# The mixture-of-experts block of layer 0 and the addition of its rows, one attention chunk earlier

## The reference

```
x = L0_attn_x
xn = _layernorm(x, axis=-1)
x = x + _L0_attn_ref(xn, ...) + _L0_ffn_ref(xn, ...)
xn = _layernorm(x, axis=-1)
x = x + _L1_attn_ref(xn, ...) + _L1_ffn_ref(xn, ...)
```

## Time and profile before

| | |
|---|---|
| median of three runs | 444.68 us (440.51 to 448.02) |
| profiled execution | 446.3 us, of it the span from first to last instruction 444.5 us |
| mean granted TensorE clock in it | 0.933 of 2.4 GHz |
| busy: PE, DVE, ACT, POOL | 363.5, 243.4, 177.2, 221.9 us |
| C2 on PE | 73.2 to 96.1 us |
| FFN of layer 0 on PE | 116.1 to 149.8 us |
| C7's last weighing on PE | 231 us |

### The profile page before, as it was taken

How to read it: one execution, slowest core, us unless ns; L and a number is a source line. 1 busy time by engine, 2 the same in 40 slices (tenths; PEclk the granted TensorE clock), 3 DMA queues, 4 the chain that set the end, 5 groups by cost and what they waited for, 6 DMA issues and landing times.

```text
span 444.5 us, 8858 instructions
## 1 busy us (share of the span) xinstructions
PE 363.5 (82%) x2609; PEld 328.5 (74%) x2623; DVE 243.4 (55%) x789; ACT 177.2 (40%) x485; POOL 221.9 (50%) x282
## 2 busy tenths in 40 slices
PE   1777878799899978979897757999999999999600
PEld 0556777597799977958686635899999999999600
DVE  5429877576611348667687766565443444343324
ACT  1514323243555534325453544433444443444221
POOL 9358260959555555693301214053557866554411
PEclk9989989899999999989998866999999999999955
DMA  8860000010155120000120182366888888887072
GB/s 260 256 235 0 2 1 2 0 49 0 49 165 168 41 86 1 0 1 10 40 94 6 44 282 56 108 211 189 248 272 284 263 264 295 269 255 222 24 214 75
DMA packets 28207, 56.02 MB, mean 126 GB/s; under 512 B 4192, under 2 KB 11680, under 8 KB 28160
## 3 DMA queue, kind: packets, MB, share of 16 engines
q1 hardware_dynamic: 24288, 47.19, 33.8%
q0 software_dynamic: 3872, 8.27, 5.8%
HBM read 46.59 MB, written 8.85 MB: 125 GB/s over the span
## 4 chain that ended last, share of the span: by engine, by line
PE 34%; POOL 22%; DVE 17%; issue 16%; DMA 4%; ACT 4%; SPq 1%; DVEq 0%; ACTq 0%; POOLq 0%
POOL y_rows L567 7%; POOL rows L561 7%; PE bank L1017 5%; PE bank L979 3%; PE bank L1073 3%; PE bank L1059 3%; DVE shared L1535 3%; DVE rmax L1522 3%; POOL shared L481 3%; PE bank L1001 2%; POOL shared L477 2%; PE bank L1283 2%; PE bank L989 2%; DMA xnT<-y_rows 2%; PE bank L963 2%
## 5 line engine op out<-in xcount | busy, mean ns | idle before, releaser
L1283 PE MATMUL bank<-kf,shared 128*128 128x128 f32 x624 | 76.2, 275 | 0.0
L1283 PEld LDWEIGHTS bank<-kf,shared 128*128 128x128 f32 x624 | 72.8, 192 | 0.0
L567 POOL DMA_INDIRECT y_rows<-rows,to x39 | 38.4, 984 | 52.8 <-DVE rows L1773 52.4
L1522 DVE TENSOR_REDUCE rmax<-bank 128x8 f32<-128x512 f32 (+2 forms) x48 | 30.2, 629 | 52.7 <-PE bank L989 26.4
L1017 PEld LDWEIGHTS bank<-shared 128*128 128x128 f32 x344 | 45.5, 195 | 16.2 <-issue 15.1
L1017 PE MATMUL bank<-shared 128*128 128x128 f32 x344 | 48.1, 282 | 9.3 <-DVE remn L1562 9.3
L1766 DVE SCALAR_TENSOR_TENSOR we<-bank,bcol,we 128x128 f32<-128x128 f32 x78 | 24.2, 347 | 54.8 <-ACT we L838 54.1
L561 POOL DMA_INDIRECT rows<-xn_rows,from x39 | 38.0, 974 | 29.3 <-issue 11.3
L838 ACT ACTIVATE we<-bank,bcol 128x128 f32<-128x128 f32 x78 | 24.4, 363 | 50.2 <-PE bank L1283 50.2
L1269 PE MATMUL bank<-xtT,shared 128*128 128x128 f32 x312 | 43.4, 284 | 0.9 <-ACT xtT L810 0.7
L686 ACT ACTIVATE shared<-bank 128x512 f32<-128x512 f32 (+2 forms) x48 | 26.5, 552 | 37.3 <-PE bank L1001 37.0
(11 more groups left out here) (252 smaller groups left out, 710.0 us busy)
## 6 DMA issues: line engine op xcount, KB each, us to landing
shared<-in_w1s SPq DMA_DIRECT2D x39, 512.0 KB, 4.3
shared<-in_w1s SPq DMA_DIRECT2D x39, 256.0 KB, 4.0
we<-in_we SPq DMA_DIRECT2D x8, 514.0 KB, 3.3
xn_rows<-xn SPq DMA_DIRECT2D x12, 256.0 KB, 2.3
xn<-y_rows SPq DMA_DIRECT2D x8, 256.0 KB, 4.0
x<-in_x SPq DMA_DIRECT2D x4, 256.0 KB, 3.7
y_rows<-kf POOLq DMA_DIRECT2D x4, 256.0 KB, 5.9
w1s<-in_w1s SPq DMA_DIRECT2D x2, 512.0 KB, 7.8
```

What stands on the lines that cost most here:

```text
L567: pool.indirect_dma_start(out=y1_rows, in_=ysb[:, i % 4, :], in_offset=None, out_offset=bass.IndirectOffsetOnAxis(ap=to1[:, i:i + 1].bitca ...
L1283: mm = pe.matmul(bank[(1, 3)[(k - 1) % 2]][:, P * f:P * f + P], wglb[:, (k - 1) % 4, 2 * F1 * a + P * f:2 * F1 * a + P * f + P], zT2[:, (k ...
L1522: dve.tensor_reduce(rmax[:, g % 2, :], s3, X, ALU.max).then_inc(s_max, 1)
```

## The change

The FFN of layer 0 moves between C2 and C3. With it move the two blocks of gathers on POOL: the first eight to the end of C1, the other eight to the end of C2. The addition moves to C4 and C5, the statistics of tiles 0 to 7 to C4, their `spread` to C5. `onto_stream(3)`, now in C4, gets a wait for `s_added` 2, and the statistics one for `s_x1`, because tiles 6 and 7 are written by POOL and by `onto_stream(3)` in the same chunk. No instruction of an engine is added or removed but these waits. The whole diff:

```diff
-BACK = 5
+BACK = 4
-FFN0_AFTER = 3
+FFN0_AFTER = 2
@@ onto_stream(n), on DVE
                 dve.wait_ge(s_proj, n + 1)
-                if n >= BACK:
-                    dve.wait_ge(s_added, 4)
+                if n >= BACK - 1:
+                    dve.wait_ge(s_added, 4 if n >= BACK else 2)
@@ the loop over chunks, on DVE
                 if n == BACK:
                     dve.wait_ge(s_added, 2)
+                    dve.wait_ge(s_x1, n)
                     statistics(range(0, 8))
```

## The result

| | before | after |
|---|---|---|
| median of the runs | 444.51 us (4 runs, 440.51 to 448.02) | 450.8 us (4 runs, 449.22 to 452.48) |
| profiled execution's span | 444.5 us | 449.0 us |
| ratio | | 1.0173, 95% interval 1.0092 to 1.0253 |

The ratio and its interval leave out executions more than 1.5% above the fastest of their kernel, so they need not be the quotient of the medians.

The account below looks back on a forecast made before the run. No single engine was taken as the bound; what counts is who waits last, with PE setting C2's pace. 5.7 + 1.2 + 2.3 - 0.5 = +8.7 us on 444.7 gave 453.4 us, range 448.7 to 457.5.

Parts of the forecast that it names:

- A: C2: eight gathers ahead of POOL's C2 work make `xw` late, so PE starts `values(3)` later; +5.7 us.
- rival 3: A second stall: POOL's cover at `onto_stream(3)` gone, or slower gathers; 2.4 to 3 us more, 456.3 us; chance 0.13.
- B: C2, behind the stall ahead of `values(3)`: PE's granted clock falls; +1.2 us, bounds 0 and 1.8.
- C: Heads of C5 to C7: earlier statistics and spread change PE's waits and clock; +2.3 us, C6 taken as 0.
- D: Around the FFN: C3, now first after it, waits less for `xw`, but C4 meets POOL's sequence; -0.5 us.
- E: C4: the addition and the new waits for `s_added` and `s_x1` hold nobody, cover 1.8 us; 0 us.
- Only the stall: Clock stays full in C2 and at C5's head, C4's statistics hide behind POOL; 450.0 us, chance 0.20.
- The other side: Relief of C6 and C7, 5.5 us, outweighs if gathers do not hold PE; faster, 440.8 us, chance 0.04.

Follow-up runs that it names:

- addition only: Against the kernel before, only the addition, statistics and spread one chunk earlier, FFN and gathers left in place; 444.87 us, ratio 0.9987.
- spread back: The changed kernel with the spread of tiles 0 to 7 back in C6; 452.93 us, ratio 1.0189 against the kernel before.
- the gathers behind: The changed kernel with all sixteen gathers and the routing wait behind `windows(3)` at the end of C2; 443.89 us, ratio 0.9953 against the kernel before.

## Why the prediction came out as it did

**A, the gathers: right.** Forecast: first gather 2.4 us behind `turn(12)` (75.6), `windows(3)` done at 95.5, +5.7 us. Shifted by the 4.41 us of scatter, the trace after has 75.75, 95.42 and `values(3)` at 95.56 in place of 89.98: +5.6. Moving only these gathers gave +7.0 with the clock, moving them away gave all of it back, and four of them cost about a quarter (1.9 of 7.3 us). The eight gathers took 9.9 us beside DVE's work, not more than the 10.2 before, so rival 3's slower gathers did not come. The first stall was 3.25 us and not 2.1, because PE reached `scores(16)` earlier, its clock having held this time; the second one decides, as forecast.

**B, the clock: right in place, somewhat low.** I took 1.2 of 0 to 1.8; it was 1.7 (7.89 us from `values(3)` to the end of C2's work, against 6.16). Keeping PE busy in the stalls removed exactly that from C2. I had the size of the drop right from the earlier trace rows. Some slow time did pass while PE waited, but it was that of the first stall: with it PE waited 2.34 us for `xw`, without it 3.75. Behind the second stall all of it counted. Two readings under B were wrong. The wait in the FFN's head is 1.87 us, of which the window in the earlier trace rows caught 1.1; and behind a wait of the same 1.87 us at the head of C2 the clock had fallen, so 2.38 us was not the shortest that lowered it:

```profile
81.50:83.40 1.90, 1.90 (x7) 1.42 (x7) 0.66 (x4) 0.38 (x1) 1.90 (x3) 0.50 0.00 0
```

So C2 before already held 1.7 us of slow clock. The gathers cost 7.3 us there with the clock alike on both sides (28.5 against 21.2), or with one fall that counts on each (30.2 against 22.9). The Trainium skill, "TensorE: Matmul & The Clock Gate" (HAM oscillation), tells of a kernel in which waits of some 3 to 5 us each made PE's next work start slow. Here a wait of 2.34 us did, and the upper bound for B, to which that page pointed, was the better guide for this stall. It isn't for the other waits, see below.

**C, statistics and spread: the step that failed.** The sentence "leaves PE's wait there hardly changed: 0", on the head of C6, was wrong by 3.1 us. The spread in C5 stands ahead of `shift(36)` and its delay is paid there, 1.60 us in `turn(36)`; PE arrives at the head of C6 later by as much, and DVE, relieved of the statistics, is not later. So the wait fell from 2.38 to 1.06, and the fall of the clock that the profiled execution of before had there went too. By the kernel with only the FFN moved, where the wait of 2.38 stood without a fall, the clock is 1.0 of the 3.1 and the shorter wait with what follows it 2.0. At the head of C5 the sum came out right (3.8 against 3.5) by other parts than mine: 2.33 more of waiting instead of 1.7, 1.60 for the shift instead of nothing, and no fall of the clock instead of 1.8. In all C was -0.5 instead of +2.3, and the kernel with this part alone says the same. That is 2.8 us less than forecast; the other terms missed by 0.7 us the other way, which makes 6.6 of the 8.7.

The sum C counted the clock on one side only: it added 1.8 us for a fall that might come at C5 and gave no chance to the one at C6 going. The four waits themselves changed by +2.33, +1.60, -1.32 and -0.90, together +1.7, where the forecast had +0.5. So C was too low in the waits and too high in the clock, and -0.5 is the value of two executions with these falls: without any it is +0.6, and with a fall at C5, as three other kernels had, 0.9 to 1.5 more. That the time came within 2.6 us of the forecast is partly luck in this. What it does not owe to luck is A, 5.6 of the 6.6 us.

**D and E: right in kind.** D was -0.2 of a range from -1.75 to 0 (taken: -0.5): POOL's sequence is waited for in C3 (0.93) and in C4 (0.39), as forecast. The new waits for `s_added` held nobody: POOL's addition in C4 ended at 178.40 and `onto_stream(3)` began at 180.00, a cover of 1.6 us where 1.8 were forecast. The second eight gathers and `rows_back` cost nothing, even when all sixteen stood in a row.

**The rivals.** "Only the stall" (450.0) came closer in time (0.8 us off) than the forecast, but not by its mechanism: the clock did hold at C5's head, yet it fell in C2, and the statistics did not hide. "The other side" named the true relief of C6 and C7, 4.4 us here, but as forecast it can't decide while the gathers hold PE; with them out of the way it remained hidden because C5 paid as much. Only when the DVE tasks stood in DVE's own waits was that relief won without the payment.

## What to carry to other kernels

An instruction that is cheap and off every chain is dangerous ahead of an engine's next obligations: eight gather issues of 1.27 us each cost 7 us one chunk earlier and nothing one chunk later. Before moving work on a queue, list what stands behind it there and when each is wanted; the lead that the engine has (here 3 us) is all that may be spent. Put extra work on an engine at the point where that engine itself waits for another, not at a point where its output is waited for, and when a delay moves, follow it to the first waiter instead of adding its size at the old one. And give the clock its chance on both sides of a comparison: a fall that goes away counts as much as one that comes.

## What the runs showed of the hardware

**The clock behind equal waits.** The wait at the head of C5 was 3.21 us in six kernels. L1017 after it took 1.13 us in three of them (changed kernel, addition only, spread back) and 2.04 or 2.05 in the other three; windows over that place (window, length, busy PE, PEld, DVE, ACT, POOL, granted clock, DMA) have a granted clock of 1.00 in the changed kernel and of 0.50 with the gathers behind:

```profile
187.00:190.00 3.00, 2.90 (x20) 2.72 (x21) 1.65 (x5) 1.25 (x3) 3.00 (x4) 1.00 0.02 5
```

```profile
177.30:180.90 3.60, 3.59 (x13) 3.13 (x14) 1.55 (x5) 0.38 (x1) 3.60 (x5) 0.50 0.00 0
```

Likewise the 1.87 us at the head of C2 lowered the clock before the change (C2 22.9 us) and not in the kernel with the gathers behind (21.2 us). The instructions of PE ahead of it are the same. There the engine went on at full clock:

```profile
82.51 1.13 PE L1014 MATMUL bank<-shared 128*128 128x128 f32 x8 [1.87 <-DVE remn L1559]
```

Over the thirteen traces:

| PE's wait | us | clock fell to 0.50 behind it | length it added, us |
|---|---|---|---|
| head of C2, gathers not ahead | 1.87 | in 5 of 7 traces | 1.7 |
| head of C2, gathers ahead | 1.71 | in 0 of 6 | |
| first wait in the FFN | 1.86 to 1.94 | in 2 of 13 | 1.7 |
| head of C5 | 3.21 | in 3 of 6 | 0.9 to 1.5 |
| head of C6 | 2.38 | in 3 of 4 | 1.0 |

A fall of the clock is therefore not settled by the wait's length and the order of the instructions, and a forecast can give it only a chance. What else settles it wasn't found. It may also be a part of the scatter of 5 to 10 us between executions of one kernel here; how large a part wasn't measured.

**DVE held by POOL.** `near(4)` on DVE reads two operands from SBUF. Alone it took 0.41 us. Beside POOL's copies and addition at the head of C5 it took 2.62 us in the changed kernel, 2.61 with the spread back and 2.61 with the addition only, but 1.27 with the gathers behind, 1.10 with four gathers ahead and 1.07 with PE kept busy. The long ones are in the three kernels whose clock held at C5's head, the short ones in the three whose clock fell: there DVE reached `near(4)` later in POOL's sequence, when the copies were done and the addition ran. The changed kernel:

```profile
190.92 2.62 DVE L1568 SCALAR_TENSOR_TENSOR near<-shared 128x256 f32<-128x256 f32 x1
191.14 0.43 POOL L496 TENSOR_TENSOR shared<-gkgv,cf 128x32 f32<-128x32 f32 x2
191.52 0.73 POOL L469 COPY xw<-xnT 128x256 f32<-128x256 f32 x2
192.22 1.03 POOL L514 TENSOR_TENSOR xn<-xn,r_gate 128x512 f32<-128x512 f32 x1
```

The Trainium skill, "SBUF — State Buffer" (Who interferes with whom), says that a DVE instruction with two SBUF inputs contends with a GpSimd instruction that reads SBUF. The trace agrees: `near(4)` began beside POOL's L481 and ended 0.3 us behind its L514, after two L496 and two L469 in between, six times its usual length. Whether it cost time isn't shown. PE's wait for DVE's shift later in C5 was 1.60 and 1.58 us in two kernels with the long `near(4)` and the spread behind it, and 1.02, 0.99 and 0.20 us in the three with the short one; but these are the kernels whose clock had fallen at C5's head, which made PE later as well, so the two can't be told apart. With the long one and no spread behind it there was no wait. The gathers of layer 0, in contrast, took 0.94 to 1.26 us each in all kernels.
